# Convolution and W_in as full-row products through the first layer, one scan of 1024 elements for four states

## What is computed

```python
# layer 1 (N = 64 states): the taps of its convolution are rows of cond_1024
proj = (conv_b + sum(x_pad[:, k:k+L] * conv_w[k, 0] for k in range(2))) @ Wp + bp
state = decay * state + dt * softplus(proj[..., :N])_t * (x @ Ws + bs)_t     # a recurrence over t
x1 = (tanh(proj[..., N:]) * state) @ Wo + bo                                  # rank 64, plus a bias
# layer 2 (1024 channels, 16 states)
xn = (x1 - mu) * rsqrt(var + EPS) * ln_g + ln_b
x_br, z = split(xn @ W_in)                      # 512 -> 1024 + 1024
xb = silu(conv4(x_br) + conv_b)                 # depthwise, 4 taps, causal
delta = softplus(xb @ W_delta + b_delta)
h_t = exp(delta_t * A) * h_{t-1} + delta_t * B_t * xb_t ;  y_t = sum(h_t * C_t)   # 16 states per channel
x2 = (y + xb * Dp) * silu(z) @ W_out + x1
# layer 3: a low-rank update of a 512x512 product, and a feed-forward stage with quantized weights
```

## Time and profile before

| | us |
|---|---|
| median of 3 runs | 3088.01 (3084.0 to 3090.0) |
| profiled execution: time, span | 3081.28, 3079.5 |
| VectorE busy in the span | 2829.8 (92%) |
| TensorE busy (matmuls) | 2536.5 (82%) |
| ScalarE, GpSimd busy | 1899.1, 1585.3 |
| TensorE's granted clock, mean | 0.91 |

### The profile page before, as it was taken

The page is one execution under the profiler, slowest core; times in us unless marked ns, Lnnn a source line. Parts: engine busy times, 40 slices in busy tenths (PEclk is TensorE's granted clock), DMA queues, the critical chain, the costliest instruction groups (busy, mean ns, idle before and its releaser), DMA issues. The chain is left out here.

```text
span 3079.5 us, 40037 instructions
## 1 busy us (share of the span) xinstructions
PE 2536.5 (82%) x11852; PEld 1726.5 (56%) x11852; DVE 2829.8 (92%) x4347; ACT 1899.1 (62%) x3495; POOL 1585.3 (51%) x1318
## 2 busy tenths in 40 slices
PE   7788888888888888888888787878787887699997
PEld 5566566656556555656566556656565633244443
DVE  2899999999999999999999999999999993688887
ACT  3657575757575757575757575757575743455554
POOL 0456565656565656565656565656565661122221
PEclk8788998999999999899989998999899898799999
DMA  4102020202020202010201010101010442111110
GB/s 168 48 1 69 1 69 1 70 1 69 1 70 1 69 1 70 1 66 4 67 5 66 4 67 4 66 4 67 4 66 4 195 165 83 59 62 61 61 62 24
DMA packets 44540, 152.27 MB, mean 49 GB/s; under 512 B 5141, under 2 KB 6037, under 8 KB 41246
## 3 DMA queue, kind: packets, MB, share of 16 engines
q1 hardware_dynamic: 44318, 149.63, 13.8%
HBM read 132.24 MB, written 17.37 MB: 49 GB/s over the span
## 5 line engine op out<-in xcount | busy, mean ns | idle before, releaser
L748 DVE TENSOR_TENSOR_SCAN ring<-a_ps,carry,ring 128x256 f32<-128x256 f32 x2048 | 1361.6, 725 | 0.0
L571 ACT ACTIVATE a_ps<-delta,nA 128x256 f32<-128x256 f32 x2048 | 853.8, 464 | 707.6 <-DVE ring L748 693.1
L378 POOL TENSOR_TENSOR ring<-ring,Cbc 128x1024 f32<-128x1024 f32 x512 | 1215.3, 2374 | 44.2
L912 PE MATMUL yT_ps<-ident,ring 128*128 128x128 f32 x4096 | 600.2, 296 | 321.0 <-POOL ring L378 307.4
L912 PEld LDWEIGHTS yT_ps<-ident,ring 128*128 128x128 f32 x4096 | 509.5, 153 | 413.0 <-POOL ring L378 356.8
L373 POOL TENSOR_TENSOR carry<-ring,half 128x4 f32<-128x4 f32 x512 | 165.0, 322 | 988.7 <-DVE ring L748 988.7
L738 DVE TENSOR_TENSOR ring<-u_ps,Bbc 128x1024 f32<-128x1024 f32 x512 | 618.2, 1210 | 17.3 <-PE yT_ps L912 9.7
L880 PE MATMUL work<-xb,big 128*128 128x256 f32 x2048 | 487.9, 392 | 24.2 <-ACT zs L450 24.2
L880 PEld LDWEIGHTS work<-xb,big 128*128 128x128 f32 x2048 | 393.2, 198 | 80.5 <-ACT zs L450 28.6
L674 DVE SCALAR_TENSOR_TENSOR xb<-xbr,V,xb 128x256 f32<-128x256 f32 x384 | 288.1, 815 | 0.0
L859 PE MATMUL work<-big,xT 128*128 128x512 f32 x512 | 269.4, 676 | 0.0
(11 more groups left out here) (165 smaller groups left out, 2762.6 us busy)
## 6 DMA issues: line engine op xcount, KB each, us to landing
Bbc<-bc_rows SPq DMA_DIRECT2D x64, 512.0 KB, 4.4
Cbc<-bc_rows SPq DMA_DIRECT2D x64, 512.0 KB, 3.6
xT<-in_xT SPq DMA_DIRECT2D x16, 514.0 KB, 4.8
x_rows<-x2row SPq DMA_DIRECT2D x32, 256.0 KB, 2.0
big<-in_f_w SPq DMA_DIRECT2D x2, 4096.0 KB, 20.0
xp<-x_rows SPq DMA_DIRECT2D x32, 256.0 KB, 2.7
xx<-in_x SPq DMA_DIRECT2D x32, 256.0 KB, 3.0
out_rows<-orow SPq DMA_DIRECT2D x32, 256.0 KB, 2.0
```

The lines of the kernel that those rows point to most:

```text
L378: nc.gpsimd.tensor_tensor(h, h, Cbc[:, G * g:G * g + G, :], ALU.mult).then_inc(s_hc, 1)
L571: r = nc.scalar.activation(a_ps[q % 2][:, i, :], delta[:, par, dt, :], ACT.Exp, scale=nA[:, dt, s:s + 1])
L748: r = dve.tensor_tensor_scan(ring[:, q % RING, i, :], a_ps[q % 2][:, i, :], ring[:, q % RING, i, :], carry[:, par, dt, s:s + 1], ALU.mult, ...
L912: r = pe.matmul(yT_ps[:, tt, :], ring[:, q % RING, i, P * tt:P * tt + P], ident[:, :], is_transpose=True, start=False, stop=(g == NG - 1 a ...
```

## The change

Three parts.

- **Layer 2's input through layer 1's rank.** x1 is a product of rank 64 plus a bias, so norm, W_in and the four taps can be folded: once, in step -1, the kernel makes `Mx` (for each tap 66 x 1024) and `Mz` (66 x 1024) from Wo, ln_g, ln_b, W_in and the taps. After that the front of a block takes only `y0` (66 rows by 256): TensorE turns it (`turn_y0`, L927), ScalarE scales it by 1/std (`y0scale`), TensorE turns it back (`turn_back`), ScalarE puts it behind the three columns of the block before (`y0back`), and `x` becomes 4 products (one a tap, the moving side shifted by a column) in place of 4 (one a 128 rows of D), `z` one product in place of 4. All are padded with zeros to 128 rows. The convolution on VectorE, `x1copy`, the norm, and a copy for each XB on ScalarE are gone; `stats` reads the PSUM bank of `wo`.
- **One scan.** The four scans of a group are one `tensor_tensor_scan` over 1024 elements. Column 0 of each state's `a` is zero (set once; ScalarE now writes columns 1 to 255), so the state starts afresh there, and what it starts with, `exp(delta_0 A) * carry + u_0 * B_0`, is put into column 0 of `Bbc` (column 0 of `u_ps` is 1). GpSimd computes these first columns for half the channels at a time (`first_col`, `first_sum`, turns 29 and 30 for the next block's first half, 6 and 7 for the second), ScalarE one `exp` for each (`first_exp`, turns 30 and 7), SyncE brings B_0 through DRAM, and VectorE copies them into `Bbc` (11 copies a block).
- **Loads.** `xT` is loaded as soon as `prj` has read it. In step 15 the two 4 MB weight loads `f_w1` and `f_w2` stand behind the second W_out product, ahead of the row loads of `c2_w2`; 1/8 of `f_w1` comes at the end.

```diff
+                if front and not (isinstance(k, int) and k == NBLK - 2):
+                    sp.wait_ge(full[BANK["PRJ"]], jobs_before("PRJ", k) + 1)
+                    sp.dma_start(xT[:, :, :], xT_in[bass.ds(n + 1, 1)].rearrange("a p k t -> (a p) k t"))\
+                        .then_inc(s_xload, 16)
...
                 if last:
+                    sp.wait_ge(full[BANK["WOUT1"]], jobs_before("WOUT1", k) + 1)
+                    sp.dma_start(big[0][:, 0:7 * DI], f_w1[:, 0:7 * DI]).then_inc(s_big[0], 16)
+                    sp.dma_start(big[1][:, :], f_w2).then_inc(s_big[1], 16)
...
+            def first_col(half, n, bp):
+                if half == 0:
+                    pool.wait_ge(s_b0l, 16 * n + 16)
+                pool.wait_ge(s_delta, 4 * n + 2 * half + 2)
+                pool.wait_ge(s_xb, 2 * n + half + 1)
+                wait(pool, s_first, 2 * n + half)
...
+                nc.gpsimd.tensor_tensor(a0[:, :, :], d0.to_broadcast([P, ND // 2, NS]), nA[:, lo:hi, :], ALU.mult)\
+                    .then_inc(s_a0, 1)
...
+                    if front and q == FIRST[0]:
+                        first_col(0, k + 1, 1 - par)
+                    if front and q == FIRST[0] + 1:
+                        first_sum(0, k + 1, 1 - par)
...
+                def y0scale():
+                    ps = take("YT")
+                    act.wait_ge(s_rstd, n + 1)
+                    for tt in range(NT):
+                        r = nc.scalar.activation(y0r[:, tt, 0:N0 + 1], ps[:, NY * tt:NY * tt + N0 + 1], ACT.Copy,
                                                  scale=nrm[:, 1, tt:tt + 1])
...
+                def first_exp(half, b):
+                    act.wait_ge(s_a0, 4 * (2 * b + half) + 1)
+                    v = a0[:, :, :].rearrange("p a b -> p (a b)")
+                    nc.scalar.activation(v, v, ACT.Exp).then_inc(s_a0e, 1)
...
-                next_plan = {5: [prj], 6: [prj_ln], 8: [lambda: x1copy(0)], 9: [lambda: x1copy(1)], 11: [norm],
-                             12: [lambda: turn(0), lambda: turn(1)], 14: [lambda: xcopy(0)],
+                next_plan = {5: [prj], 6: [prj_ln], 10: [y0scale], 11: [y0back], 14: [lambda: xcopy(0)],
...
+                    if front and q == FIRST[0] + 1:
+                        first_exp(0, k + 1)
...
-                        dve.wait_ge(free[BANK[f"WO{tt}"]], jobs_before(f"WO{tt}", k) + 1)
-                        dve.bn_stats(stat[:, tt, :], xn[:, tt, :]).then_inc(s_stat, 1)
+                        dve.wait_ge(full[BANK[job]], jobs_before(job, k) + 1)
+                        dve.bn_stats(stat[:, tt, :], work[BANK[job]][:, :]).then_inc(free[BANK[job]], 1)
...
+                    if g == 0 and dt in (0, ND // 2):
+                        dve.wait_ge(s_first, 2 * k + (2 if dt else 1))
+                    if dt == 0:
+                        dve.tensor_copy(Bbc[:, G * g:G * g + G, 0], first[:, 0, G * g:G * g + G]).then_inc(s_col0, 1)
+                        dve.wait_ge(s_col0, NCOL * k + g + 1)
+                    elif g == 0:
+                        dve.tensor_copy(Bbc[:, :, 0], first[:, dt, :]).then_inc(s_col0, 1)
+                        dve.wait_ge(s_col0, NCOL * k + NG + dt)
...
-                    for i in range(G):
-                        s = G * g + i
-                        r = dve.tensor_tensor_scan(ring[:, q % RING, i, :], a_ps[q % 2][:, i, :],
-                                                   ring[:, q % RING, i, :], carry[:, par, dt, s:s + 1],
-                                                   ALU.mult, ALU.add)
-                    r.then_inc(s_scan, 1)
+                    dve.tensor_tensor_scan(ring[:, q % RING, :, :].rearrange("p g t -> p (g t)"),
+                                           a_ps[q % 2][:, :, :].rearrange("p g t -> p (g t)"),
+                                           ring[:, q % RING, :, :].rearrange("p g t -> p (g t)"), 0.0,
+                                           ALU.mult, ALU.add).then_inc(s_scan, 1)
...
-                        7: [("b", wout, 1, 0)], 8: [("b", wout, 1, 1)], 9: [("b", wout, 1, 2)], 10: [("n", turn)],
+                        7: [("b", wout, 1, 0)], 8: [("b", wout, 1, 1)], 9: [("b", wout, 1, 2), ("n", turn_y0)],
+                        10: [("n", turn_back)],
...
+                    if isinstance(k, int) and k == -1 and q == 7:
+                        make_m()
+                    if isinstance(k, int) and k == -1 and q == 11:
+                        turn_m()
```

More of the change, by code:

```diff
@@ L28 @@
 RANK = 8
+NY = N0 + 2
 EPS = 1e-5
@@ L147, in scan_phase @@
         yT_ps = pb("yT_ps", [P, NT, P])
+        abank = [a_ps[i // 2][:, 2 * (i % 2):2 * (i % 2) + 2, :].rearrange("p a b -> p (a b)") for i in range(4)]
         u_full = pb("u_ps", [P, 512])
@@ L760, in step @@
                 for q in range(NQ):
+                    if isinstance(k, int) and k == -1 and q == 12:
+                        mx_scale()
+                        dve.memset(u_ps[:, 0:1], 1.0).then_inc(s_aclr, 1)
+                        dve.wait_ge(s_mxc, ND)
+                        for i in range(2):
+                            dve.memset(a_ps[i][:, :, 0:1], 0.0).then_inc(s_aclr, 1)
                     for job in (scan_plan.get(q, []) if scan else []):
@@ L788, in _ @@
             r.then_inc(s_biasmm, 1)
+            pe.wait_ge(s_ident, 1)
+            pe.wait_ge(s_woc, 3)
+            for d in range(KD):
+                r = pe.transpose(abank[0][:, P * d:P * d + N0 + 1], Woc[:, P * d:P * d + P], ident[0:N0 + 1, 0:N0 + 1])
+            r.then_inc(s_wot, 1)
             pe.wait_ge(s_setD, 8)
-            pe.wait_ge(s_ident, 1)
             def step(k, par, front, back, scan):
@@ new lines, in turn_back, with make_m @@
+                def turn_back():
+                    ps = give("YB")
+                    pe.wait_ge(free[BANK["YT"]], jobs_before("YT", k) + 1)
+                    for tt in range(NT):
+                        r = pe.transpose(ps[0:NY, P * tt:P * tt + P], y0r[:, tt, :], ident[:, :])
+                    r.then_inc(full[BANK["YB"]], 1)
+                def make_m():
+                    weights(3)
+                    pe.wait_ge(s_wog, 2)
+                    for half in range(2):
+                        for m in range(4 * half, 4 * half + 4):
+                            for d in range(KD):
+                                r = pe.matmul(abank[half][:, NY * (m % 4):NY * (m % 4) + NY], Win[:, d, P * m:P * m + P],
+                                              WoTg[:, d, :], start=(d == 0), stop=(d == KD - 1))
+                        r.then_inc(s_mxt, 1)
+                    for c in range(2):
+                        for d in range(KD):
+                            r = pe.matmul(abank[2 + c][0:NY, :], WoTg[:, d, :],
+                                          Win[:, d, DI + 512 * c:DI + 512 * c + 512],
+                                          start=(d == 0), stop=(d == KD - 1))
+                        r.then_inc(s_mz, 1)
@@ new lines, in turn_m @@
+                def turn_m():
+                    for m in range(ND):
+                        pe.wait_ge(s_mxs, m + 1)
+                        if m < 2:
+                            pe.wait_ge(s_mzc, m + 1)
+                        else:
+                            pe.wait_ge(s_mxc, m - 1)
+                        for tap in range(4):
+                            r = pe.transpose(abank[2 + m % 2][0:NY, P * tap:P * tap + P], MTk[:, m, tap, :], ident[:, :])
+                        r.then_inc(s_mxp, 1)
```

280 lines of the change are left out of this document (157 added, 123 removed).

## The result

| | us |
|---|---|
| before, median of 4 runs | 3086.0 (3083.6 to 3090.0) |
| changed, median of 4 runs | 3009.4 (3005.3 to 3013.0) |
| ratio, with its 95% interval | 0.975 (0.973 to 0.977) |
| forecast | 2906 (2735 to 3030) |

The change is faster by 77 us. The forecast was 180 us: right in its direction and inside its range, but over twice too much.

A forecast was written before the change was run, and what follows sets the result against it. VectorE was taken as the bound, busy 154.5 of a block's 155.25 us. A block: 155.0 - 30.7 + 18.1 = 142.4; the run: 3081.3 - 176 - 19 + 6 + 12 = 2904, plus 2 gives 2906 us, range 2735 to 3030.

The forecast's parts named there:

- The convolution: VectorE's convolution leaves its list: 18.6 us a block.
- step 15: Last step: weight loads ahead of the row loads make TensorE wait up to 20 us, VectorE 13; 6 more in all.
- eleven copies at 4.4 a block: VectorE's copies into column 0 of Bbc: 2.2 us for all eleven, plus 2.2 for turn 0's wait behind GpSimd's product.
- turn 30 at 4.9: VectorE stalls 4.9 us a block: first_exp waits for GpSimd, then zsilu and table loads precede turn 30's exponentials.
- the start: Before the first scan: folding Wo, make_m and transposes, less z products, cost 12 us, with 5 and 20 as ends.
- the stall of turn 10: VectorE waits for y0scale and exponentials behind TensorE's queue: 3.5 to 4.7 us a block, taken as 4.7.
- two product steps an element: Long scan at 2.08 ns an element lasts 2.32 us, saving 11.5 us a block; the other end gave 7.0.
- A fixed part that differs by 49 ns between two operations is nothing odd: Reason for accepting a scan's fixed part of 192 ns beside a product's 143, and so 2.32 us.
- Elsewhere [...] the copy [...] gets in ahead of it: nothing: Outside turn 0, the copy after u starts before GpSimd's product and so costs no wait.
- the copies are locked out: Rival, chance 0.10: seven copies behind u each wait 2.2 us for GpSimd's product; 246 us, total 3150.
- The rival of more gaps and a lower clock: Chance 0.15: new stalls idle TensorE, its clock drops, another 5 to 8 us a block; near 149 a block, 3000.
- The rule cited with the forecast: VectorE and GpSimd share a port pair under an exclusive lock; whoever starts first holds it for the whole instruction.

The follow-up runs named there:

- e8: Changed kernel without its scan part: four scans of 256 from carry, no copies into column 0, no first columns; 2948.2 us, 0.956.
- e4: Changed kernel with step 15's f_w2 load back at the step's start and f_w1 behind the row load of chunk 2; 2992.8 us, 0.970.
- e5: Changed kernel with its scan of 1024 elements cut into four of 256, each from 0.0; 3051.7 us, 0.989.
- e9: Kernel before the change with its four scans a group started from 0.0, state not carried over; 2975.9 us, 0.965.
- e1: Changed kernel with the copies into column 0 moved to the start of their turns, ahead of dmin, dmax and u; 2937.7 us, 0.952.
- e2: Changed kernel with zsilu ahead of first_exp in ScalarE's turn 30; 2956.5 us, 0.958.
- e3: Changed kernel with turn_y0 moved to TensorE's turn 8, ahead of wout's last three products; 2964.5 us, 0.961.
- e7: Changed kernel with the moves of e1 to e4 together, and a block's first u computed in turn 31 of the block before; 2769.2 us, 0.897.
- e10: Kernel before the change with one scan of 1024 from 0.0 a group, carries left out, no copies; 2979.4 us, 0.966.

## Why the forecast was right in its mechanism and wrong in its size

**The convolution: right.** The forecast without its scan part (scans -184, eleven copies at 4.4 a block +70, turn 30 at 4.9 for 15 blocks +73, together -41) is 2906 + 41 = 2947; e8 took 2948.2. Within it, the start was sized too small (12, though its own terms, 3 + 16 + 6 less 10.8, make 14; the trace shows 22.3) and step 15 as well (6; e4 took 17 off), and the stall of turn 10 too large (4.7; 3.5). That these nearly cancel is luck.

**The scan: right as a sum, wrong in its reason.** 2.32 us forecast, 2.28 measured; 184 forecast, 197 measured. But I put all of it down to fixed parts of three scans saved. e5 and e9 show that 124 us of it (1361.6 to 1237.5) are the start value, which is no longer read from SBUF, and only 73 the length. The choice of two product steps an element was right (2.10 ns against 1.04). "A fixed part that differs by 49 ns between two operations is nothing odd" was where I stopped asking: 187 ns of fixed part are 127 and 60 for the operand.

**The copies: the step that failed.** "Elsewhere [...] the copy [...] gets in ahead of it: nothing" was worked out for turn 3 and held for the turns that have only `u` ahead of the copy. It was not worked out for those with a `dmax` or `dmin` in front (turns 2 and 27), nor for one that waits for TensorE first (turn 15). Forecast 70 us, measured 154.9 with their waits, 85 more. Some 55 of them are copies held by GpSimd's product: turn 2 in 16 blocks (35), turn 27 in 5 (10) and turn 15 in 9 (10). The rest, some 30, are waits for TensorE, most of which e8 has as well. The rival "the copies are locked out" had the mechanism, but counted seven copies of each block behind `u`; the trace has turn 15's and turn 27's of these in some of the blocks, and turn 2's, which it did not count, in all.

**`u` and `dmin`: not costed at all.** They are held behind GpSimd as a copy is, and added copies shift them: 31 us for the scan part in the changed kernel, 22 of them the `u` of turn 27 in 10 blocks, and 34 more for `u` in e1. The sum asks what GpSimd does beside the new instructions, but not beside the old ones that now stand elsewhere.

**The stalls of turns 10 and 30: right,** in place and cause. Turn 30: 78.6 us more of waits ahead of scans between e8 and the changed kernel for a forecast of 73; e2 took back 53. Turn 10 is in e8 too, and e3 took back 45. It came at 3.46 us, the forecast's bound without a low clock (3.5). TensorE's granted clock does drop, to a mean of 0.66 from 1038 to 1043 us, behind a wait of 2.74 us for `stats`, but it is 1.00 in the 14 us that follow, and the 1.2 us that the forecast added to the stall for it do not show.

**The rival of more gaps and a lower clock** named 3000 us, near the result, but not by its mechanism: the window from 900 to 2300 us has a mean granted clock of 0.90 in the changed kernel and 0.90 in e8, which is 61 us faster.

Together: the scan part was forecast at -41 and came at +57 to +61, which is 98 to 102 of the 103 us between forecast and result.

The rule cited with the forecast holds and goes further than I used it. In the Trainium skill ("SBUF — State Buffer", section SBUF: two separate sides) the shared ports are taken not only by operations in a two-port mode but also by a VectorE operation with two SBUF inputs, against a GpSimd operation that reads SBUF. `u` reads `delta` and `xb` and lasts 0.42 us ahead of the product and 2.57 behind it (changed kernel and e1), as that says, while the product over `u_ps` and `Bbc`, one input of which lies in PSUM, keeps its 1213 ns beside GpSimd's.

What stays open: which of the remaining 79 us of waits for TensorE in e7 could go, with the 18 ahead of its first copies, and whether a `u` that is never held in turn 27 would give e10 its 30 us. No run moves it there: e10's lost 73 us are accounted for by the sum above and not by a test.

## What to carry to other kernels

Before an instruction is added to an engine that another one can hold, walk every turn it stands in and ask what runs on the other engine at that moment, for it and for whatever it pushes back; a 0.15 us copy cost 2.3 behind a product and nothing beyond its own length right behind the scan that the product waits for. When an engine has been full and a change takes a fifth off its list, price the change by the next waits and not by the list: four small moves in the order were worth more than twice the change itself. Try the halves of a change apart: here one half earned 138 us and the other lost 61, until it was placed well and earned 112.

## What the runs showed of the hardware

- A scan whose start value is a column in SBUF lasts 725 ns for 256 elements, from a constant 665: 60 ns for the operand, 124 us over 2048 scans. Its slope is 2.10 ns an element.
- A copy of 4 elements a partition takes 0.15 us and up to 2.34 behind a GpSimd product; a product of two SBUF operands over 255 elements 0.42 and 2.57. VectorE's `dmax` in turn holds GpSimd: its carry of four elements takes 0.20 us alone and 0.63 to 0.74 behind it.
- Who starts first decides, and by very little: over the changed kernel, e9 and e10, `u` in turn 27 lasts 2.57 us or more in all 25 blocks in which the carry starts ahead of `dmax` (by 0.02 to 0.10 us), and 0.43 or less in all 20 in which it starts behind (by 0.01 to 0.13). In e10 this took 30 of the 73 us that the long scan saves.
